# Seven single PSUM banks in one pool, score tiles read in halves, and one rotary product in place of two

## What is computed

```python
for i in range(6):                              # layers
    xn = adaln(x, cond, n1_w[i], n1_b[i])
    q, k, v = split(xn @ qkv_w[i].T, 3)
    x = x + attn(rope(q), rope(k), v) @ so_w[i].T          # 16 heads of 8, 512 keys
    xn = adaln(x, cond, n2_w[i], n2_b[i])
    q, k, v = rope(xn @ cq_w[i].T), rope(ctx @ ck_w[i].T), ctx @ cv_w[i].T
    x = x + attn(q, k, v) @ co_w[i].T                      # 77 keys
    xn = adaln(x, cond, n3_w[i], n3_b[i])
    x = x + gelu(xn @ f1_w[i].T + f1_b[i]) @ f2_w[i].T + f2_b[i]
# rope, on the 8 features of a head: x1, x2 = halves of 4
#   (x1 * cos - x2 * sin,  x1 * sin + x2 * cos)
# attn: softmax(q k / sqrt(8)) with the row maximum subtracted first
```

## Time and profile before

| | |
|---|---|
| median of 3 runs | 2342.19 us (2342.07 to 2351.33) |
| the profiled execution's own time | 2346.46 us |
| its span | 2344.7 us |
| PE busy | 1883.7 us, 80% of the span |
| DVE busy | 1655.5 us, 71% |
| ACT busy | 1483.1 us, 63% |
| POOL busy | 929.8 us, 40% |
| mean granted clock of TensorE | 0.904 of full speed |

### The profile page before, as it was taken

How to read it: one execution, slowest core, us unless ns; L and a number is a source line. 1 busy time by engine, 2 the same in 40 slices (tenths; PEclk the granted TensorE clock), 3 DMA queues, 4 the chain that set the end, 5 groups by cost and what they waited for, 6 DMA issues and landing times.

```text
span 2344.7 us, 36580 instructions
## 1 busy us (share of the span) xinstructions
PE 1883.7 (80%) x13318; PEld 798.6 (34%) x13318; DVE 1655.5 (71%) x3027; ACT 1483.1 (63%) x1840; POOL 929.8 (40%) x1420
## 2 busy tenths in 40 slices
PE   3564381167899999999999999999999999988651
PEld 2333271012233333333333333333334333333321
DVE  7766011367788887888878887888888887786456
ACT  2442020035678878878887877888877887767442
POOL 2443705123244453444444344444444445423421
PEclk9776696579999999999999999999999999989765
DMA  2001121322233433323433324432432333411100
GB/s 95 1 1 42 49 96 47 85 55 63 59 71 83 92 81 89 76 55 82 105 86 70 83 64 88 91 83 69 97 80 60 76 93 87 90 38 37 33 6 9
DMA packets 153713, 156.45 MB, mean 67 GB/s; under 512 B 32247, under 2 KB 137523, under 8 KB 153523
## 3 DMA queue, kind: packets, MB, share of 16 engines
q1 hardware_dynamic: 151487, 149.91, 27.1%
q0 software_dynamic: 2048, 4.20, 0.6%
HBM read 83.73 MB, written 67.85 MB: 65 GB/s over the span
## 4 chain that ended last, share of the span: by engine, by line
PE 58%; DVE 14%; ACT 4%; issue 4%; POOL 1%; DMA 1%; SPq 0%; POOLq 0%; DVEq 0%; ACTq 0%
PE ps L1328 14%; PE ps L1292 7%; DVE smax L1826 6%; PE ps L1281 6%; PE ps L1406 6%; PE ps L1447 4%; PE ps L1438 4%; PE ps L1340 4%; ACT big L1561 2%; PE ps L1381 2%; DVE rot L1842 2%; PE ps L1365 2%; PE ps L1303 1%; PE ps L1315 1%; PE ps L1398 1%
## 5 line engine op out<-in xcount | busy, mean ns | idle before, releaser
L1561 ACT ACTIVATE big<-ps 128x1024 f32<-128x1024 f32 x960 | 956.2, 1027 | 258.8 <-PE ps L1292 240.2
L1826 DVE TENSOR_REDUCE smax<-ps 128x2 f32<-128x1024 f32 x768 | 921.7, 1221 | 261.5 <-PE ps L1281 255.7
L1328 PE MATMUL ps<-big,vaug 128*32 128x512 f32 x3072 | 412.1, 615 | 2.9 <-ACT big L1561 2.9
L1281 PE MATMUL ps<-k,q 49*128 49x512 bf16 x1536 | 294.1, 391 | 64.3 <-DVE smax L1826 35.5
L1292 PE MATMUL ps<-q,k 52*128 52x512 bf16 x1536 | 295.4, 387 | 12.1 <-DVE smax L1826 5.6
L1757 POOL CAST mparts<-smax 128x16 bf16<-128x16 f32 x96 | 19.5, 203 | 569.1 <-DVE smax L1826 569.1
L1281 PEld LDWEIGHTS ps<-k,q 49*128 49x128 bf16 x1536 | 72.7, 94 | 310.5 <-DVE smax L1826 105.4
L1406 PE MATMUL ps<-xnT,w 128*128 128x512 f32 x288 | 166.8, 665 | 0.9 <-ACT xnT L1598 0.9
L1833 DVE TENSOR_REDUCE maxima<-ps 128x8 f32<-128x616 f32 x192 | 144.6, 795 | 31.6 <-PE ps L1315 30.0
L1292 PEld LDWEIGHTS ps<-q,k 52*128 52x128 bf16 x1536 | 75.2, 94 | 195.0 <-issue 90.2
L1748 POOL TENSOR_TENSOR hat<-rot,rparts 128x512 f32<-128x512 f32 x72 | 83.6, 1161 | 112.2 <-ACT rparts L1609 112.2
(11 more groups left out here) (302 smaller groups left out, 2877.4 us busy)
## 6 DMA issues: line engine op xcount, KB each, us to landing
q<-scratch_queries SPq DMA_DIRECT2D x48, 384.0 KB, 5.6
k<-scratch_keys SPq DMA_DIRECT2D x48, 384.0 KB
cq<-scratch_cross_queries SPq DMA_DIRECT2D x48, 384.0 KB, 6.3
scratch_queries<-rparts SPq DMA_DIRECT2D x24, 384.0 KB, 2.4
scratch_keys<-rparts SPq DMA_DIRECT2D x24, 384.0 KB, 2.6
scratch_cross_queries<-rparts SPq DMA_DIRECT2D x24, 384.0 KB
scratch_queries<-rparts SPq DMA_DIRECT2D x24, 256.0 KB, 2.7
scratch_keys<-rparts SPq DMA_DIRECT2D x24, 256.0 KB, 2.8
```

The costliest lines, as they stand in the source:

```text
L1281: last = nc.tensor.matmul(out[:, u], m.q6[rows, v % 2, 2 * g + pr, qt * P:(qt + 1) * P], m.k6[rows, v % 2, 2 * g + pr, :], start=True, sto ...
L1328: last = nc.tensor.matmul(m.ps[32 * j:32 * j + 32, pv_bank, :], of_head(m.vaug, v % 2 * TB + kt, g, j), of_quad("self", q)[:, j, :], start ...
L1561: nc.scalar.activation(of_quad(kind, p // 2)[:, p % 2 * 2:p % 2 * 2 + 2, :], banks("exp" if kind == "self" else "cross exp", p), ACT.Exp, ...
L1826: nc.vector.tensor_reduce(m.smax[:, n % 2, qt, :, pr], banks("max", i), AX.X, ALU.max).then_inc(s_read["self"], 1)
```

## The change

1. **One pool of single banks.** Banks 0 to 6 become seven single banks, given by the same `shared` to all uses, those of `aux` among them; a tile of 128x1024 takes two of them, which need not be neighbours. Bank 7 is that of the weighted values. `free_bank` waits for the last user of that one bank. In the table of the uses, the second half of a tile ends 1/8 of a unit after the first, so the halves of a tile can go to different users.
2. **Halves.** Each exponential is two ACT instructions of 128x512 and each maximum two DVE reductions, of 128x512 or 128x308, and each half signals for itself. The last block's `copy_hidden` is also two copies, with one signal. The feed-forward's first product takes four single banks, each freed by its own GELU.
3. **One rotary product.** The weights with swapped columns are gone, and so is the second product. DVE writes the product with the two halves of each head exchanged (`stream_shuffle`, lanes i and i xor 4) to the second half of the buffer, and in a second instruction the product times cos to the first half. POOL now first multiplies the second half with the sines and then adds. The keys of the context are done at once, in one product of 308 columns.
4. The places of all steps that remain are as they were. The single product has the place of the second one before.

```diff
-    pv_bank, aux = 6, 7
+    banks, pv_bank = 7, 7
...
+    def each(kind, taken, given, count, parts=2, every=1):
+
+        return [(at(taken, every * i), at(given, i) + u / 8, (kind, i, u)) for i in range(count) for u in range(parts)]
...
-            def free_banks(kind, i):
+            def free_bank(kind, i, u=0):
 
-                if ring_before[kind, i] is not None:
-                    before, j = ring_before[kind, i]
-                    freed, per = ring_freed[before]
-                    pe.wait_ge(freed, per * (j + 1))
-                return banks(kind, i)
+                if bank_before[kind, i, u] is not None:
+                    before, n, half = bank_before[kind, i, u]
+                    freed, per = bank_freed[before]
+                    pe.wait_ge(freed, n + 1 if per == 1 else 2 * n + half + 1)
+                return bank(kind, i, u)
+
+            def free_pair(kind, i):
+                return [free_bank(kind, i, u) for u in range(2)]
...
-                nc.scalar.activation(of_quad(kind, p // 2)[:, p % 2 * 2:p % 2 * 2 + 2, :], banks("exp" if kind == "self" else "cross exp", p),
-                                     ACT.Exp, scale=scale).then_inc(probs[kind], 1)
+                for u in range(2):
+                    nc.scalar.activation(of_quad(kind, p // 2)[:, p % 2 * 2 + u, :], bank("exp" if kind == "self" else "cross exp", p, u),
+                                         ACT.Exp, scale=scale).then_inc(probs[kind], 1)
...
-                nc.vector.tensor_reduce(m.smax[:, n % 2, qt, :, pr], banks("max", i), AX.X, ALU.max).then_inc(s_read["self"], 1)
+                for u in range(2):
+                    nc.vector.tensor_reduce(m.smax[:, n % 2, qt, u, pr:pr + 1], bank("max", i, u), AX.X, ALU.max).then_inc(s_read["self"], 1)
...
-                nc.vector.tensor_tensor(m.rot[:, rot[kind, i]], banks(kind, i), m.cs[:], ALU.mult).then_inc(x_read[kind], 1)
+                out, product = m.rot[:, rot[kind, i]], bank(kind, i)
+                nc.vector.stream_shuffle(out[:, 1, :], product, OTHER_HALF)
+                nc.vector.tensor_tensor(out[:, 0, :], product, m.cs[:, 0, :], ALU.mult).then_inc(x_read[kind], 1)
...
             def rotate(kind, i):
-                pool.wait_ge(x_read[kind], 2 * (i + 1) if kind == "context" else i + 1)
+                pool.wait_ge(x_read[kind], i + 1)
                 x = turned(kind, i)
+                if kind == "context":
+                    other = x[:, 1, :].rearrange("p (b n) -> p b n", n=N_CTX)
+                    r_chain.link(nc.gpsimd.tensor_tensor(other, other, m.cs[:, 1:2, 0:N_CTX].to_broadcast([P, B, N_CTX]), ALU.mult))
+                else:
+                    r_chain.link(nc.gpsimd.tensor_tensor(x[:, 1, :], x[:, 1, :], m.cs[:, 1, :], ALU.mult))
                 nc.gpsimd.tensor_tensor(x[:, 0, :], x[:, 0, :], x[:, 1, :], ALU.add).then_inc(x_rot[kind], 1)
```

281 lines of the change are left out of this document (140 added, 141 removed).

## The result

The changed kernel takes 2380.51 us (median of 4 runs, 2378.59 to 2384.01), the kernel before beside it 2346.76 (4 runs, 2342.07 to 2351.66). The ratio is 1.0145, with a 95% interval of 1.0114 to 1.0176: slower by 34 us, where a gain had been forecast. The time lies just above the forecast's range, which ended at 2378. The profiled execution took 2384.0 us, its span is 2382.3.

A forecast was written before the change was run, and what follows sets the result against it. PE was taken as the limit (67.7 of a 70 us visit), ACT and DVE having 13 us spare each. Per visit -1.06+0.8-0.6 = -0.86, times 24 -21, context -5: 2346.5 to 2320.5, less 4.3 to the median: 2316 us, range 2250 to 2378.

The forecast's parts named there:

- POOL. +1.27 us for each of three, 3.8 in 29.6, no limit.: POOL's added multiplication in a visit's three rotary turns: 3.8 us more beside 29.6 busy, not limiting.
- cross product: One cross-query product less, once a visit near 1352 us: PE's stream moves up by the whole 1.06 us.
- pool of banks: PE's 0.89 us wait at a visit's start: single banks come back 0.6 us earlier, counted -0.6 us a visit.
- context's step: Context keys, once a layer: one product of 308 columns saves 0.9 us, about 5 us in six layers.
- Queries and keys: Their saved products, 2.1 us of PE a visit, meet an ACT no earlier because of POOL's later sum: counted 0.
- The late rounding of the cross queries: ACT's rounding there comes 1.0 us late behind POOL; idle time covers it, counted 0, otherwise 1.0 us a visit.
- Exponentials in halves: ACT's full stretch from 1326.78: 0.10 us more each, PE 0.8 us late at the cross values.
- Maxima in halves: DVE: 0.09 us more each, 3 to 4 us a visit, parallel to ACT in the full stretch, counted 0.
- The shuffle: DVE's new rotary instruction, three times a visit: 688 ns taken, +0.09 us each beside PE's work.
- PE keeps all it saves: Rival: earlier products pull ACT's full stretch forward, the visit loses 3.2+0.6 us: 2246 us, chance 0.20.
- The halves cost more and ACT takes over: Rival, stretch from 1326.78: gains gone at 0.17 us per exponential, 2374 us at 0.30; chance 0.24.
- It cancels: Rival: the cross queries' late rounding (1.0 us) reaches PE and takes the cross product's gain: about 2340 us, chance 0.20.

The follow-up runs named there:

- rotary_no_mult: Kernel before with single rotary products and shuffles, the multiplication by the sines left out; banks in pairs, exponentials and maxima whole: 2328.87 us, ratio 0.9932.
- cross_single_late: cross_single with ACT's first rounding of the cross queries later in its order: 2343.16 us, ratio 0.9987 to the kernel before.
- halves_only: Kernel before with exponentials and maxima each in two instructions, the pair of banks freed after the second: 2369.17 us, ratio 1.0088.
- pool_halves: Changed kernel with the old two-product rotary step, DVE's step in two instructions; single-bank pool and halves kept: 2361.45 us, ratio 1.0061 to the kernel before.
- cross_single: Kernel before with one product, a shuffle and POOL's multiplication for the cross queries alone: 2363.59 us, ratio 1.0070.
- no_cross_mult: Changed kernel without POOL's multiplication in the cross queries' turn alone: 2378.92 us, ratio 1.0123 to the kernel before.
- exp_halves_only: Kernel before with exponentials in two instructions, the pair of banks freed after the second, maxima whole: 2358.38 us, ratio 1.0045.
- max_halves_only: Kernel before with maxima in two instructions, the pair of banks freed after the second, exponentials whole: 2356.49 us, ratio 1.0043.
- rotary_only: Kernel before with single rotary products, shuffles and POOL's multiplication; banks in pairs, exponentials and maxima whole: 2390.35 us, ratio 1.0176.

## Why the prediction was wrong

The direction was wrong. One step failed with most of the time: **"POOL. +1.27 us for each of three, 3.8 in 29.6, no limit."** Without that multiplication the changed kernel takes 2327 us in place of 2381, so the term that was counted as no limit is worth 54 us, 42 of them in the turns of queries and keys. The prediction had set the late sum of these against 2.1 us of PE's products, and had read from a share of 29.6 in 70 us that nothing more could come of it. A second step hid behind the first: that 2327 lies near the forecast of 2316 is luck. If PE kept what the prediction says it saves, the kernel without the multiplication would also keep the 2.1 us a visit that were set against it, some 50 us more; in rotary_no_mult it kept 0.42 of 3.2.

Four terms, per visit or for 24 visits, set against what the runs measured:

| step | forecast | measured |
|---|---|---|
| cross product | -1.06, -25 us | 0 (cross_single_late) |
| both halvings | +0.8, +19 us | +0.76 (halves_only) |
| pool of banks | -0.6, -14 us | +0.20 (pool_halves less halves_only), +5 us |
| context's step | -5 us | third visit +3.2 us, 6 layers, +19 us (the change less pool_halves) |

Three of the four are off by 25, 19 and 24 us, 68 together; the forecast missed by 64. Per visit the measured column gives 0+0.76+0.20+3.2/4 = 1.76 us, against 1.89 in the profiles. Both sums come close, but they prove little, since the terms were measured in different kernels: the first row is 0 only with the rounding moved, and +0.67 without (cross_single).

**"Cross queries (1.06 us ...) PE's stream moves up by the whole 1.06."** This step failed. The visit takes 69.26 us against 69.21 once the late rounding is out of the way. That PE carries 58% of the chain says that PE's work is on the path, not that all of a piece taken out is gained. DVE has 13 us of spare time in a visit and is still what PE meets next: in cross_single_late it starts a maximum only when PE has made its scores (idle for 0.47 us at 1356.07), and PE needs that maximum's banks at once.

**"Context keys ... I take 5."** This step failed too. The product itself gave what was forecast or more: the third visit takes 68.97 us in rotary_no_mult and 70.23 before, 1.26 less, of which up to 0.4 can be the other products' (as in the fourth visit); 0.9 was forecast. But POOL's "no limit" was read from 29.6 of 70 us. Three turns follow each other on POOL in that visit, and their multiplications, 3.3 us together, stand in front of the context's sum, for which ACT waits with exponentials behind the rounding. I had costed the context without its place in POOL's queue.

**"Queries and keys (2.1 us) ... I count 0 here."** The net was right in ordinary visits: 69.8, 69.3 and 70.9 us in the change, 69.6, 69.1 and 70.8 in pool_halves. The multiplication costs 1.1 us there and the products give as much, half of the 2.1 us that the prediction let cancel. The miss is in the third visit, above.

**The late rounding of the cross queries: "I count 0; without that cover it is 1.0 us a visit."** In the changed kernel the multiplication of this turn costs 0.23 us a visit (no_cross_mult, 70.87 against 71.10; 2 us by the medians, and the intervals overlap), so 0 was nearly right there. With only this turn changed the late rounding costs 0.62 us a visit, 20 us: the 0.39 and 0.35 us of idle time did not cover ACT's wait of 1.05 (at 1372.10 in cross_single), and PE waited up to 0.7 us for a pair of banks (13.1 us in all at L1439). Why the changed kernel hides it was not tested.

**Exponentials in halves.** Forecast 0.10 us each and 0.8 us a visit; measured 0.05 to 0.06 each and 0.34 a visit. The prediction's place for it, the cross values at the end of ACT's full stretch, shows no wait for ACT in exp_halves_only. By the Trainium skill (VectorE: DVE Perf Modes, "The TRN2 errata") each ScalarE instruction that reads PSUM pays 172 cycles, an estimated 0.143 us. That is more than twice what the second instruction cost here as a mean of the group. That section of the Trainium skill advises tiles of at least 512 elements, which the halves still have, so its advice does not speak against them as the prediction had it.

**Maxima in halves.** Forecast 0.09 us each and 0 on the path; measured 0.06 (2x795.8/1257 = 1.27 against 1.20 by the earlier trace rows) and 0.50 us a visit. A smaller size and a larger effect. That "the two run in parallel" did not hold, because PE waits for maxima at several places of a visit: of what its idle time there grows in max_halves_only, 0.33 us a visit, only 0.08 is where it already waited. The rest of the 0.50 was not followed. The sum of both halvings came out right by luck: one was forecast 0.46 too high, the other 0.50 too low.

**Pool of banks, -0.6 us a visit.** This step failed: the visit is 0.20 us longer in pool_halves than in halves_only, and PE's wait is 1.02 to 1.04 us where it was 0.89. The +0.20 is not the pool's alone, since pool_halves has one DVE instruction more in each turn, and its turns take two banks where those of the change take one. By the table the third maximum of a visit takes two banks whose reader is planned to end earliest, both halves of an earlier maximum, while in the run another bank was free sooner. That reading of the table was not tried in a run, so it is argued only and the cause stays open. Where the single products' multiplication is left out, the pool and the halves cost nothing together (68.80 against 68.79 us). So their price depends on what else is on the path, and the parts don't add up: 21 us for the halves and 41 for the rotary step alone (by the ratios) are more than the 34 of all.

**The shuffle.** Forecast 688 ns, measured 731, and some 14 ns more for the load of its mask. By the Trainium skill (VectorE: DVE Perf Modes, "The perf-mode tier table") it has only the slow mode, an estimated 0.7 us here, and the trace agrees.

**The rivals.** "PE keeps all it saves" (2246) is ruled out by rotary_no_mult: even without POOL's multiplication 0.42 of 3.2 us a visit was kept. "The halves cost more and ACT takes over" gave 2374 and the right side, but by the wrong mechanism: a pair is at 0.05 where it would have decided from 0.17. "It cancels" named a late rounding that reaches PE, the right mechanism, but at the cross queries and not at the queries, keys and context keys. The last sign that the forecast named came true: "If PE's new idle time is released by POOL's or DVE's rotary steps, my count of 0 there was the error." It was, through ACT: POOL's sum held ACT's rounding, and ACT's exponentials held PE (30.0 us at L1291).

## What to carry to other kernels

Count a new instruction at every place where its engine's queue is dense, not against the engine's share of a visit: the short multiplications on POOL, busy for 43% of the span, cost 1.1 us in an ordinary visit and 4.0 where three turns follow each other. A microsecond taken from the engine that carries the chain is worth what the next release allows, so look at the piece behind it and at whose buffer that needs: here 1.06 us of PE became 1.09 us of waiting. Where an engine takes its work in order, a late input of a side step costs as much as the work queued behind it is urgent, and moving the side step in the order can be worth more than the operation removed: 20 us in cross_single, where the product less gave nothing.

## What was not expected of the hardware

The granted clock in the ramp, while the first visits fill the engines, differs between the kernels. The windows from 500 to 600 us of before, of the change and of cross_single_late:

```profile
500.00:600.00 100.00, 77.31 (x494) 22.60 (x492) 72.33 (x83) 61.35 (x74) 31.95 (x53) 0.93 0.34 78
```

```profile
500.00:600.00 100.00, 76.80 (x430) 20.46 (x422) 66.36 (x128) 57.69 (x111) 34.55 (x55) 0.78 0.34 74
```

```profile
500.00:600.00 100.00, 76.43 (x489) 22.21 (x488) 72.06 (x85) 60.23 (x71) 32.72 (x53) 0.93 0.34 74
```

With 0.78 PE did 430 instructions in the same 77 us of busy time in which it did 494 at 0.93; the two mixes are not quite the same, as the change has fewer products. In steps of 10 us the change is at 0.50, the lower of the clock's two levels (1.2 GHz), from 580 to 590, right after a step in which PE was busy for 4.2 us; the kernel before is at 1.00 (2.4 GHz) there. This may be part of the 9 us that the change lost before its first full visits (the first GELU at 685.04 in place of 675.79); how much was not measured. Nor is it known what comes first, the lower clock or the later work: each kernel has one profile, and all of them lie between 0.72 (rotary_only) and 0.93.
